# Maximum by difference on ScalarE, and value matmuls issued in pairs, in the second layer of a two-layer network

## The reference, cut to what matters

```python
ss, sd = sigmoid(x @ Ws), sigmoid(x @ Wd)          # gates, top 3 of 5 kept
q = einsum('bthed,bthe->bhtd', (x @ Wq), sd_g)
k = einsum('bthed,bthe->bhtd', (x @ Wk), ss_g)
v = einsum('bthed,bthe->bhtd', (x @ Wv), ss_g)
attn = softmax(einsum('bhid,bhjd->bhij', q * scale, k), axis=-1)
out = einsum('bhij,bhjd->bihd', attn, v)
x = x + einsum('bthem,bthe->btm', (out @ Wo), md)
```

## Time and profile before

| what | value |
|---|---|
| median of 3 runs | 1859.26 us |
| lowest and highest run | 1854.18 and 1868.14 us |
| profiled execution, first to last instruction | 1857.2 us |
| TensorE busy | 1645.3 us, 8612 matmuls |
| VectorE busy | 1435.4 us |
| ScalarE busy | 782.5 us |
| GpSimd busy | 878.0 us |
| TensorE's mean granted clock | 0.945 of full speed |

### The profile page before, as it was taken

One profiled execution on the slowest core, in us unless ns is written; L12 is line 12 of the kernel. 1 busy time (PEld: TensorE's weight loads), 2 busy tenths in 40 slices (PEclk: granted clock), 3 DMA queues, 4 the chain that ended last, 5 costly groups with the idle time before them and its releaser, 6 DMA issues.

```text
span 1857.2 us, 26270 instructions
## 1 busy us (share of the span) xinstructions
PE 1645.3 (89%) x8612; PEld 999.3 (54%) x8612; DVE 1435.4 (77%) x2387; ACT 782.5 (42%) x1046; POOL 878.0 (47%) x906
## 2 busy tenths in 40 slices
PE   3899999999999672699899899899999899899997
PEld 2555555555554361566466466466565565565554
DVE  4996785785786369888888888888898888988862
ACT  3457557567556320223433434334334234234441
POOL 2710000000000024358678589589588587687654
PEclk9799999999999775889899999999999999999996
DMA  2000000000000000000000000000000000000000
GB/s 58 1 1 1 1 1 1 1 1 1 1 1 1 11 1 11 0 11 1 11 1 2 11 1 1 11 1 1 12 1 1 11 1 1 1 1 1 1 11 13
DMA packets 12224, 9.34 MB, mean 5 GB/s; under 512 B 3840, under 2 KB 11584, under 8 KB 12096
## 3 DMA queue, kind: packets, MB, share of 16 engines
q1 hardware_dynamic: 12096, 7.66, 1.5%
HBM read 6.61 MB, written 1.05 MB: 4 GB/s over the span
## 4 chain that ended last, share of the span: by engine, by line
PE 66%; DVE 19%; issue 7%; POOL 5%; ACT 2%; SPq 0%; DMA 0%; DVEq 0%; POOLq 0%; ACTq 0%
PE ps L786 10%; PE ps L606 8%; PE ps L623 7%; PE ps L638 7%; PE ps L759 6%; PE ps L581 5%; PE ps L775 4%; PE ps L776 4%; DVE den L1283 3%; PE ps L747 3%; DVE mxp L1256 3%; PE ps L749 2%; PE ps L748 2%; POOL z L1398 2%; PE ps L797 2%
## 5 line engine op out<-in xcount | busy, mean ns | idle before, releaser
L960 ACT ACTIVATE pbuf<-ps 128x1024 f32<-128x1024 f32 x256 | 262.1, 1024 | 524.0 <-PE ps L776 520.9
L1074 DVE TENSOR_REDUCE mxp<-ps 128x1 f32<-128x512 f32 (+3 forms) x560 | 354.2, 671 | 112.2 <-PE ps L606 56.2
L1256 DVE TENSOR_REDUCE mxp<-ps 128x1 f32<-128x512 f32 x512 | 342.5, 682 | 66.8 <-PE ps L759 66.1
L875 ACT ACTIVATE pbuf<-ps 128x1024 f32<-128x1024 f32 (+3 forms) x320 | 281.7, 896 | 199.1 <-PE ps L626 98.5
L1283 DVE TENSOR_TENSOR den<-den,pbuf 128x704 f32<-128x704 f32 x224 | 292.0, 1303 | 1.1
L786 PE MATMUL ps<-pbuf,h_v 128*64 128x512 f32 x1024 | 284.4, 634 | 0.0
L759 PE MATMUL ps<-k1T,q1T 128*128 128x512 f32 x512 | 223.4, 453 | 38.7 <-DVE mxp L1256 25.1
L1383 POOL TENSOR_TENSOR den<-den,pbuf 128x320 f32<-128x320 f32 x224 | 235.0, 1049 | 42.1 <-ACT pbuf L960 26.5
L606 PE MATMUL ps<-kM,qT 128*128 128x512 f32 (+3 forms) x640 | 243.6, 427 | 9.5 <-ACT kM L862 4.3
L1238 DVE TENSOR_TENSOR gt<-ps,gate 128x320 f32<-128x320 f32 x384 | 182.6, 484 | 54.8 <-PE ps L749 51.7
L623 PE MATMUL ps<-qT,kM 128*128 128x512 f32 (+3 forms) x640 | 207.7, 399 | 8.4 <-ACT pbuf L875 8.4
(11 more groups left out here) (212 smaller groups left out, 2484.3 us busy)
## 6 DMA issues: line engine op xcount, KB each, us to landing
wraw<-in_Wkv SPq DMA_DIRECT2D x16, 160.0 KB, 2.6
wraw<-in_Wq SPq DMA_DIRECT2D x8, 160.0 KB, 2.3
out<-x SPq DMA_DIRECT2D x4, 256.0 KB, 2.3
wqkv<-in_wqkvT SPq DMA_DIRECT2D x1, 192.0 KB, 4.0
masks<-in_masks SPq DMA_DIRECT2D x1, 128.0 KB, 4.1
dft<-in_dft SPq DMA_DIRECT2D x1, 128.0 KB, 2.3
wout<-in_Wo SPq DMA_DIRECT2D x2, 64.0 KB, 2.6
ident<-in_ident SPq DMA_DIRECT2D x1, 64.0 KB, 5.7
```

The source lines that it names most:

```text
L875: nc.scalar.activation(pbuf0[:, u % NP0, :, off:CH], ps[:, b:b + 2, off:CH], ACT.Exp, scale=float(D0) ** -0.5).then_inc(s_exp, 1)
L1074: v.tensor_reduce(mxp[:, i, h:h + n, b], ps[:, ring0.bank(step), 0:w * n].rearrange("p (h k) -> p h k", h=n), AX.X, ALU.max).then_inc(s_re ...
L1256: v.tensor_reduce(mxp1[:, it % TPC, b:b + 1], ps[:, ring1.bank(step), :], AX.X, ALU.max).then_inc(s_read1d, 1)
```

## The change

The change has two parts, both in the second layer.

The maximum. GpSimd computes `kd`, the difference between the first and the second 512 keys of each 1024 (pair p of a head, two a head, step "kd"). For each query tile and pair there are still two matmuls of 512 columns: "dif" with `kd`, and "max" with the second keys. ScalarE clamps "dif" at zero into one of two buffers `relu`, and VectorE adds that to "max" and keeps the maximum over the 512 columns, in one instruction: q·b + max(q·(a-b), 0) = max(q·a, q·b). `mxp1` has two columns where it had four. "dif" of the next pair is issued ahead of "max" of this one. The difference of the next head overwrites that of the present one, so GpSimd first waits for its last use. "dif" uses the ring of three banks and is read by ScalarE.

The value matmuls. At every odd u, "V" of steps u-3 and u-2 are issued one behind the other; at even u there is none. "D" stays at u-2 in every step.

To make room in SBUF the small constants of the parts before share their place with the new buffers, and `sq2` has 65 columns instead of 128.

```diff
@@ preparation1
             out += [(end + STAGE1[2] + 0.3 * w, ("t", h, c, w)) for w in range(3)]
+            if c % 2:
+                out.append((end + STAGE1[2] + 0.65, ("kd", h, c // 2)))
...
-            items = [("max", h, TPC * c + i, b) for i in range(TPC) for b in range(NC)]
+            pairs = [(h, TPC * c + i, p) for p in range(NC // 2) for i in range(TPC)]
+            items = [("dif", *pairs[0])]
+            for a, b in zip(pairs, pairs[1:] + [None]):
+                items += [("dif", *b)] if b else []
+                items.append(("max", *a))
@@ foreground1
             if 0 <= u - 2 < U1 * H1:
-                seq += [("V", u - 2), ("D", u - 2)]
+                if u % 2:
+                    seq += [("V", u - 3), ("V", u - 2)]
+                seq.append(("D", u - 2))
@@ rings
-        ring1 = Ring(SEQ1, ("proj", "max", "F", "y"), ("t", "q2", "zt"))
+        ring1 = Ring(SEQ1, ("proj", "max", "F", "y"), ("t", "dif", "q2", "zt"))
+        PAIR1 = [step[1:] for step in SEQ1 if step[0] == "dif"]
+        SLOT1 = {pair: i for i, pair in enumerate(PAIR1)}
@@ TensorE
-                elif kind == "max":
-                    _, h, it, b = step
+                elif kind in ("dif", "max"):
+                    _, h, it, p = step
                     bank = take(ring1, step)
                     wait_read(pe, ring1, ("t", h, NC - 1, 2))
-                    pe.matmul(ps[:, bank, :], q1T[:, h % 2, P * it:P * (it + 1)],
-                              k1T[:, h % 2, CH * b:CH * (b + 1)], start=True, stop=True).then_inc(s_turn1, 1)
+                    if kind == "dif":
+                        pe.wait_ge(s_kd, NC // 2 * h + p + 1)
+                        keys = kd[:, p, :]
+                    else:
+                        keys = k1T[:, h % 2, CH * (2 * p + 1):CH * (2 * p + 2)]
+                    pe.matmul(ps[:, bank, :], q1T[:, h % 2, P * it:P * (it + 1)], keys,
+                              start=True, stop=True).then_inc(s_turn1, 1)
@@ ScalarE
+                elif kind == "dif":
+                    i = SLOT1[step[1:]]
+                    wait_turn(act, ring1, step)
+                    if i >= NR:
+                        wait_read(act, ring1, ("max", *PAIR1[i - NR]))
+                    nc.scalar.activation(relu[:, i % NR, :], ps[:, ring1.bank(step), :],
+                                         ACT.Relu).then_inc(s_read1a, 1)
@@ VectorE
                 elif kind == "max":
-                    _, h, it, b = step
+                    _, h, it, p = step
+                    above = relu[:, SLOT1[h, it, p] % NR, :]
                     wait_turn(dve, ring1, step)
-                    v.tensor_reduce(mxp1[:, it % TPC, b:b + 1], ps[:, ring1.bank(step), :],
-                                    AX.X, ALU.max).then_inc(s_read1d, 1)
+                    wait_read(dve, ring1, ("dif", h, it, p))
+                    v.tensor_tensor_reduce(above, ps[:, ring1.bank(step), :], above, 1.0, LOW, ALU.add, ALU.max,
+                                           accum_out=mxp1[:, it % TPC, p:p + 1]).then_inc(s_read1d, 1)
@@ GpSimd
+                elif step[0] == "kd":
+                    _, h, p = step
+                    wait_read(pool, ring1, ("t", h, 2 * p + 1, 0))
+                    if h:
+                        wait_turn(pool, ring1, ("dif", h - 1, NT - 1, p))
+                    a, b = (k1T[:, h % 2, CH * (2 * p + i):CH * (2 * p + i + 1)].bitcast(F32) for i in range(2))
+                    g_.tensor_tensor(kd[:, p, :], a, b, ALU.subtract).then_inc(s_kd, 1)
```

More of the change, by code:

```diff
@@ L46 @@
 NS = 2
+NR = 2
+LOW = -3e38
 M1 = NT // 2
@@ L182, in build @@
         ones = sbuf(ctx, "ones", [P, 1])
-        wgate = sbuf(ctx, "wgate", [P, 2, H1 * E1])
         wout = sbuf(ctx, "wout", [P, 3, D])
[L185 to L192, removed]
+        small = ExitStack()
+        sm = lambda name, shape, dt=F32: sbuf(small, name, shape, dt)
+        wgate = sm("wgate", [P, 2, H1 * E1])
+        wlin = sm("wlin", [P, 4, D])
+        blin = sm("blin", [P, 3, D])
+        bqcol = sm("bqcol", [P, 1])
+        stdp = sm("stdp", [P, 3, H0])
+        blockm = sm("blockm", [P, D])
+        bd = sm("bd", [P, 2, D])
+        bsum = sm("bsum", [P, H0])
+        lden = sm("lden", [P, 2, TPC, H0])
+        small.close()
+        relu = sbuf(ctx, "relu", [P, NR, CH])
+        kd = sbuf(ctx, "kd", [P, NC // 2, CH], F32R)
+        sq2 = sbuf(ctx, "sq2", [P, TPC, D1 + 1])
         l0 = ExitStack()
@@ L273, in build @@
         rd1 = s1("rd1", [P, TPC])
-        mxp1 = s1("mxp1", [P, TPC, NC])
+        mxp1 = s1("mxp1", [P, TPC, NC // 2])
         mx1 = s1("mx1", [P, TPC])
@@ L278, in build @@
         sq1 = s1("sq1", [P, TPC, P])
-        sq2 = s1("sq2", [P, TPC, P])
         k1T = s1("k1T", [P, 2, T], F32R)
@@ L340, in build @@
         s_st1 = sem("s_st1")
+        s_kd = sem("s_kd")
         s_m1 = sem("s_m1")
@@ L412, in build @@
         ring0 = Ring(SEQ0, ("max", "F", "pj", "mix", "lin"), ("k", "q", "q2", "at", "lt", "lt2"))
-        ring1 = Ring(SEQ1, ("proj", "max", "F", "y"), ("t", "q2", "zt"))
+        ring1 = Ring(SEQ1, ("proj", "max", "F", "y"), ("t", "dif", "q2", "zt"))
+        PAIR1 = [step[1:] for step in SEQ1 if step[0] == "dif"]
+        assert PAIR1 == [step[1:] for step in SEQ1 if step[0] == "max"]
+        SLOT1 = {pair: i for i, pair in enumerate(PAIR1)}
         def wait_read(eng, ring, step):
```

## The result

The changed kernel takes **1890.14 us** (median of 4 runs, 1886.74 to 1891.87); the kernel before took 1858.97 in the same comparison (4 runs, 1854.18 to 1868.14). The ratio is 1.017, with a 95% interval of 1.0135 to 1.0205: 31 us slower, where the forecast was 51 us faster. The profiled executions have spans of 1888.2 and 1857.2 us.

A forecast was written before the change was run, and what follows sets the result against it. The prediction took TensorE's stream to bound the last head, and that stream plus waits a middle head. It summed 44 + 14 + 3 - 10 = 51 us off 1857.2, giving 1806 us, range 1760 to 1845.

The forecast's parts named there:

- (f): Order: in even steps VectorE's normaliser addition no longer lies beside value matmuls; priced at 0, up to 34 us.
- (b): VectorE's maxima: 32 combined instructions of 0.75 us replace 64 reductions, saving 20 us a head of VectorE's time.
- (e): GpSimd's two key subtractions a head, 1.30 us each: priced at 0, 35 us without the buffers' cover.
- (a): Paired value matmuls on TensorE: 0.35 us less per pair, 44 us in all, all on the path.
- (c): VectorE's relief on the path: 14 us of waits for late VectorE go, and 3 us in head 0's opening.
- the 127.0 of the prediction: Length of a middle head after the change, in us: 133.2 - 5.6 - 2.0 + 1.4.
- the stalls that "stay": Six stalls of 3.9 us behind the weights' split (23.5) and six of 1.4 behind z (8.6), expected unchanged.
- (d): ScalarE's 32 clamps a head at 0.60 us: 10 us of waits return, bounds 0 and 30; clamp-released waits under 15.
- the first (the new order eats the relief, 1861): Waits of the new order 65 us in place of 10, no change; almost no gain, 1841 to 1878, had chance 0.16.
- "stalls of the chain": Slower than 1878 us by these stalls or a combined instruction of over 1.9 us: chance 0.06.

The follow-up runs named there:

- e5: Kernel before with paired value matmuls alone, and the normalisation of a query tile, with its addition to z, one step later: 1857.85 us, ratio 1.0001.
- e10: Kernel before, values in every step, with the normalisation of a query tile one step later: 1842.04 us, ratio 0.9914.
- e12: Changed kernel with the split of the next head's weights two steps earlier: 1843.41 us, ratio 0.9922.
- e15: Changed kernel with the weights split two steps earlier and the normalisation of a query tile one step later: 1821.38 us, ratio 0.9811.
- e8: Kernel before with only the split of the next head's weights two steps earlier: 1825.35 us, ratio 0.9826.
- e16: Kernel before with the weights split two steps earlier and the normalisation of a query tile one step later: 1843.32 us, ratio 0.9931.
- e6: Kernel before with paired values alone, the even steps' normaliser addition half a step later, directly ahead of the next scores: 1887.08 us, ratio 1.0148.
- e1: Kernel before with the paired value matmuls alone, the maximum still with four reductions on VectorE: 1909.81 us, ratio 1.0267.
- e13: Kernel before with the maximum by difference alone, the first key subtraction issued on GpSimd behind the last projected tile's sum: 1859.70 us, ratio 1.0012.
- e3: Changed kernel with both key subtractions on VectorE instead of GpSimd, the first three steps later: 1887.10 us, ratio 1.0148.
- e17: Changed kernel with weights split two steps earlier and the first key difference behind the last projected tile's sum: 1834.09 us, ratio 0.9888.
- e2: Changed kernel with values issued every step as before, so the maximum by difference alone: 1876.81 us, ratio 1.0088.
- e14: Kernel before with the maximum by difference alone and the normalisation of a query tile one step later: 1826.56 us, ratio 0.9841.

## Why the prediction was wrong, step by step

**The step that failed is (f), the order.** It priced the bare addition of the even steps at 0, from a load of VectorE per step (3.3 us against 3.7; the 94 us of (b) would make it 2.9), and gave 34 as its bound. The pair alone costs 53, and 13 on top of the difference. Taking z one step away gives 38 more with the pairs than without (e5 against e10), 40 more on the whole change (e12 to e15 against e8 to e16), and moving the additions alone 23 (e6). On average VectorE has room, but not in the step whose addition z holds for 3.35 us in place of about 0.9. The value step had been part of that addition's cover: without it TensorE has some 0.8 us less to do there (e1).

**(e) GpSimd failed too, at its place and not at its load.** It was priced at 0 with 31 us idle per head and a bound of 35. The wait forecast was there (1.55) and so was the work (1.30), but the step looked at the buffers of the exponentials and of the projected tiles, not at the last tile of the head, whose sum stands on the path through ScalarE to the query row. In the difference alone this is 17 of 20 us (e13). In the whole change TensorE waits 12.8 us for that row too, but nothing ties this to the subtraction: e3 and e17 took ScalarE's wait for the sum from 11.0 to 6.4 and left the 12.8 as it was, and e6, without any subtraction, has the same 12.8. Its cause stays open.

**(a) Right in its size, wrong on the path.** 0.35 per pair is exact, and no price of a pair was hidden in it. "All on the path, since the stream is the path" is true of the last head only. In a middle head TensorE waits for VectorE, and the value matmuls are what it waits behind. Even with the addition to z moved, the pair costs 1857.9 - 1842.0 = 16 us; where these come from was not settled (in e5 19.2 us of waits for the maxima's rows and 17.5 for products are left, in e10 6.2 and 13.7).

**(b) Right:** 0.77 against 0.75, and 96 us of VectorE per head against 94. The Trainium skill (VectorE: DVE Perf Modes, Two Vector instructions with no wait between them) has two instructions for an operation that writes its accumulator. The trace agrees, with 0.08 for the second.

**(c) Not gained as the change was made.** The 14 us were the waits of the earlier trace rows for products, 8.7 and 5.6. In e2, where VectorE has 18 us a head less to do and the order of the values is the old one, they are 8.7 and 8.3: these waits did not go with VectorE's load. The 3 us of the opening were there (4.3). With the normalisation later, the difference gives 1842.0 - 1826.6 = 15.5 us against 14 + 3 forecast, but that is luck in part: the waits for products fall only from 19.6 to 16.4 us there. The middle head of 126.7 meets the 127.0 of the prediction by luck too, since the 127.0 counted 5.6 for the pairs, which e14 does not have; beside e10's 128.2 it is 1.5 less. With the pairs, the stalls that "stay" grew from 23.5 to 27.9 us and from 8.6 to 9.9. The early split (e8) shows what they really cost: 32 us, where the earlier trace rows has 23.5.

**(d) The clamp** takes 0.60, and waits released by it are 4.9, under the 15 named. TensorE's waits for ScalarE in all rose from 4.9 to 23.6, not by 10. More than half of that is the query row, whose cause in the whole change is open.

**The clock was in no term.** After a stall the matmuls run in part at the lower level. From 790 to 1755 us 17 of the 111 pairs that the trace shows lasted 2.6 to 3.7 us in place of 1.94 (those behind the split all did), 22.8 us in all. Before, seven value steps lasted 1.98 in place of 1.08, six of them behind the split, 6.3 us in all. So some 16 of the 40.8 us by which the seven heads grew lie in the slower value matmuls alone, behind the longer stalls.

**Of the rivals,** the first (the new order eats the relief, 1861) had the mechanism and too low a price. Slower by "stalls of the chain" had a chance of 0.06, far too small when the bounds of (d), (e) and (f), 20 + 35 + 34 over the forecast, already reach 1895.

## What to carry to other kernels

An engine's mean load says nothing of a step in which one of its instructions is held: look up its longest instructions, ask what they run beside, and what of the neighbour's work covers them. Independent matmuls that look like overhead are also the cover of such a hold; bundling them saves their entries and takes the cover away from every second step. And before a change that is to relieve an engine, part the instructions that hold each other: here one number in the plan was worth 32 us on the kernel before, where the change beside its own best neighbour brought 4, which the intervals do not tell from nothing.

## What the runs showed of the hardware

VectorE does not share with GpSimd here, it stands still. After, around the meeting of the split with z:

```profile
1326.58 2.35 POOL L1436 TENSOR_TENSOR onm<-on,maskd 128x1280 f32<-128x1280 f32 x1 [7.16 <-DVE on L1327]
1329.01 3.17 POOL L1440 TENSOR_TENSOR z<-z,onm 128x1280 f32<-128x1280 f32 x1
...
1327.02 2.42 DVE L1263 CAST wh<-wraw 128x960 fp32r<-128x960 f32 x1
1329.48 3.71 DVE L1264 TENSOR_TENSOR wl<-wraw,wh 128x960 fp32r<-128x960 f32 x1
```

Apart from z, in e10, the same two take 1.16 and 0.65:

```profile
L1231 DVE TENSOR_TENSOR wl<-wraw,wh 128x960 fp32r<-128x960 f32 x5 | 5.8, 1159 | 0.2
L1230 DVE CAST wh<-wraw 128x960 fp32r<-128x960 f32 x5 | 3.2, 649 | 0.0
```

The cast ends 0.51 us after GpSimd's product, the subtraction 1.01 after GpSimd's addition, and the held addition of the normaliser 0.76 after its one (1227.11 against 1226.35): each about its own undisturbed time or a little under it. So each waited for the whole of GpSimd's instruction and then ran. The Trainium skill (SBUF — State Buffer, Who interferes with whom) states such an exclusive lock between the two engines. The trace agrees. It also shows the other side: in e2 an addition of VectorE started 0.17 us ahead of GpSimd's addition to z (1288.86 above), and it was GpSimd's that grew, to 3.52 from 2.9:

```profile
1288.69 0.89 DVE L1316 TENSOR_TENSOR den<-den,pbuf 128x704 f32<-128x704 f32 x1
```

The prediction had taken 3.73 for a property of the subtraction, to which nothing could be done.

TensorE's clock was the other surprise. A gap of 1.41 left the next matmuls at full speed; gaps of 0.70 and 1.64, 3.5 us apart, left a pair at 3.01. The length of the last gap does not decide it: after, a gap of 2.08 left the pair behind it at 3.02 at 848 us, and one of 2.07 left it at 1.94 at 1268 us. The kernel that waits less also runs faster while it works: a granted clock of 1.00 over the middle head of e14, 0.94 in e1.
